# Column sums over half the rows: h's two row blocks added up ahead of TensorE, and the search's steps placed anew

## Time and profile before

| | |
|---|---|
| median of 3 runs | 497.21 us |
| the profiled execution | 497.13 us |
| its span, first to last instruction | 495.3 us |
| TensorE matmul busy | 476.9 us, 96% |
| VectorE busy | 371.3 us, 75% |
| GpSimd busy | 364.2 us, 74% |
| ScalarE busy | 354.4 us, 72% |
| DMA queue of SyncE, share of the 16 engines | 54.1% |
| granted TensorE clock | 1.00 |

### The profile page before, as it was taken

How to read it: one execution, slowest core, us unless ns; L and a number is a source line. 1 busy time by engine, 2 the same in 40 slices (tenths; PEclk the granted TensorE clock), 3 DMA queues, 4 the chain that set the end, 5 groups by cost and what they waited for, 6 DMA issues and landing times.

```text
span 495.3 us, 7476 instructions
## 1 busy us (share of the span) xinstructions
PE 476.9 (96%) x2442; PEld 327.1 (66%) x2442; DVE 371.3 (75%) x948; ACT 354.4 (72%) x727; POOL 364.2 (74%) x343
## 2 busy tenths in 40 slices
PE   1999999999999999999999999999999999999996
PEld 0256577667776777767776777757776677777774
DVE  5997898989887887789887897779876675533334
ACT  4767999877778777777788687768877665555652
POOL 0266569958789688868878687877879687797873
PEclk9999999999999999999999999999999999999999
DMA  8992556456566465646666266646444143444424
GB/s 320 339 411 90 225 199 238 148 217 245 214 236 255 171 243 214 238 164 267 255 254 253 94 263 253 245 180 243 185 179 168 76 163 128 158 171 169 171 85 169
DMA packets 27718, 102.75 MB, mean 207 GB/s; under 512 B 2080, under 2 KB 2592, under 8 KB 27680
## 3 DMA queue, kind: packets, MB, share of 16 engines
q1 hardware_dynamic: 27296, 101.23, 54.1%
q0 software_dynamic: 384, 1.05, 0.5%
HBM read 68.72 MB, written 33.55 MB: 206 GB/s over the span
## 4 chain that ended last, share of the span: by engine, by line
PE 82%; DVE 7%; ACT 4%; DMA 3%; issue 2%; POOL 1%; SPq 0%; DVEq 0%; ACTq 0%; POOLq 0%
PE ps L671 46%; PE ps L677 21%; PE aux L633 4%; PE ps L699 4%; PE aux L730 3%; DVE stats L804 2%; DMA xin<-x 2%; DVE res L986 1%; ACT hb L336 1%; PE aux L620 1%; PE aux L657 1%; DMA xg<-x_t,rows 1%; POOL h_lo L526 1%; PE aux L644 1%; ACT h_hi L372 1%
## 5 line engine op out<-in xcount | busy, mean ns | idle before, releaser
L537 POOL TENSOR_TENSOR r_lo<-r,r_hi 128x512 fp32r<-128x512 f32 x128 | 163.8, 1302 | 50.2 <-ACT r_hi L409 48.7
L526 POOL TENSOR_TENSOR h_lo<-hb,h_hi 128x512 fp32r<-128x512 f32 x128 | 164.3, 1297 | 7.3 <-ACT h_hi L372 7.3
L986 DVE SCALAR_TENSOR_TENSOR res<-ps,bias,res 128x512 f32<-128x512 f32 x128 | 90.0, 745 | 68.4 <-PE ps L706 68.4
L671 PE MATMUL ps<-r_hi,w_hi 128*128 128x512 f32 x256 | 108.0, 422 | 0.1
L671 PE MATMUL ps<-h_hi,w_hi 128*128 128x512 f32 x256 | 105.2, 411 | 0.5 <-DVE res L986 0.5
L671 PE MATMUL ps<-r_hi,w_lo 128*128 128x512 f32 x256 | 101.1, 395 | 0.0
L671 PE MATMUL ps<-h_hi,w_lo 128*128 128x512 f32 x256 | 101.1, 395 | 0.0
L336 ACT ACTIVATE hb<-xin,nmean,rstd 128x1024 f32<-128x1024 f32 x64 | 78.6, 1229 | 7.5 <-DVE nmean L825 7.3
L804 DVE BATCH_NORM_STATS2 stats<-xin 128x6 f32<-128x512 f32 x128 | 79.3, 677 | 4.1 <-DMA xin<-x 4.1
L392 ACT ACTIVATE r<-ps,beta 128x512 f32<-128x512 f32 x64 | 43.4, 684 | 53.2 <-PE ps L699 52.8
L386 ACT ACTIVATE r<-ps,beta 128x504 f32<-128x504 f32 x64 | 43.5, 679 | 51.6 <-PE ps L699 51.1
(11 more groups left out here) (101 smaller groups left out, 550.4 us busy)
## 6 DMA issues: line engine op xcount, KB each, us to landing
res<-x SPq DMA_DIRECT2D x32, 1024.0 KB, 4.9
out<-res SPq DMA_DIRECT2D x31, 1024.0 KB, 4.0
xin<-x SPq DMA_DIRECT2D x30, 1024.0 KB, 7.2
xin<-x SPq DMA_DIRECT2D x4, 512.0 KB, 5.4
out<-res SPq DMA_DIRECT2D x4, 256.0 KB, 2.1
w<-w_t SPq DMA_DIRECT2D x1, 256.0 KB, 9.5
cst<-small SPq DMA_DIRECT2D x1, 229.5 KB, 7.2
xg<-x_t,rows POOLq DMA_INDIRECT x8, 5.2
```

The source lines that it names most:

```text
L526: last = nc.gpsimd.tensor_tensor(h_lo[:, kf, n], hb[:, b % NH, kf, n], h_hi[:, kf, n].bitcast(F32), ALU.subtract)
L537: last = nc.gpsimd.tensor_tensor(r_lo[:, kf, n], r[:, kf, n], r_hi[:, kf, n].bitcast(F32), ALU.subtract)
L671: nc.tensor.matmul(bank[m][:], wt[:, kf, m * P:m * P + P], mov[:, kf, n], start=(kf == 0 and wt is w_hi), stop=False, skip_group_check=True)
L986: nc.vector.scalar_tensor_tensor(res[:, b % NR, m, n], bank[m][:], bias2[:, m:m + 1], res[:, b % NR, m, n], ALU.add, ALU.add).then_inc(out ...
```

## The change

- From group 3 on (`is_folded`), h's two row blocks are added up first, into a new tile `h_sum` [128, 4, 1024], and `column_sums` makes 16 matmuls on it where it made 32 on `hb`.
- For the first and the last batch of a group, VectorE adds the blocks (`add_blocks`, one 128x1024 fp32 instruction): the group's first batch in the third iteration, between `group_counts` and `moments`; its last batch in the first iteration of the next four, between `table` and `finish(t, 0)`.
- For the two in the middle, ScalarE writes h's first block a second time into `h_sum` (`write_twice`, ahead of `normalise` in the second and third iteration), and GpSimd issues a DMA that adds the second block to it in SBUF (`fold`, first thing in the third and fourth iteration).
- `column_sums` moves behind `layer2(t, 1)`, for all groups; `take_sums` moves behind `split_h(t+2, 0)`.
- `top_rows` moves from the end of the first iteration to the second, ahead of `finish(t, 0)`; `top_mark` behind that `finish`; `codes` moves from the second iteration to the third, ahead of `finish(t, 0)`, `group_onehot` to behind it.
- VectorE's `group_twin` goes; ScalarE's `twin` does both halves, in the third and the fourth iteration.
- `gather` moves from GpSimd's first iteration (last place) to the second, ahead of `split_h(t+2, 1)`. `transposes` and `spread_counts` move from the third to the fourth, and so does `group_gathered`.

```diff
--- before.py
+++ after.py
@@ -114,6 +114,7 @@
         r = sb("r", [P, KF, N])
         r_hi = sb("r_hi", [P, KF, N], F32R)
         r_lo = sb("r_lo", [P, KF, N], F32R)
+        h_sum = sb("h_sum", [P, G, N])
         fv = sb("fv", [P, N + 8])
         code = sb("code", [P, N], BF16)
         code_r = sb("code_r", [P, N], BF16)
@@ -208,6 +209,8 @@
         norm_ready = sem("norm_ready")
         h_part = sem("h_part")
         h_ready = sem("h_ready")
+        folded = sem("folded")
+        added = sem("added")
         fv_done = sem("fv_done")
         fv_copied = sem("fv_copied")
         static_ready = sem("static_ready")
@@ -260,6 +263,11 @@
             return k if (t + 1) % G == step and 1 < k < GROUPS else None
 
 
+
+        def is_folded(b):
+            return 3 * G <= b < NB
+
+
         def nth(b, h):
             return 2 * b + h + 1
 
@@ -393,6 +401,13 @@
                                                 accum_out=src2[:, m, e, NCLS:NSRC], **com)
                 last.then_inc(r_ready, 1)
 
+            def write_twice(b):
+                e = b % RB
+                act.wait_ge(norm_ready, b + 1)
+                act.wait_ge(fv_done, 2 * (b // G))
+                nc.scalar.activation(h_sum[:, b % G], xin[:, b % NX, 0], ACT.Relu, bias=nmean[:, 0, e:e + 1],
+                                     scale=rstd[:, 0, e:e + 1])
+
 
             def first_unit():
                 for m in range(KF):
@@ -487,11 +502,10 @@
                 relu(t + 1, 0, 0)
                 relu(t + 1, 0, 1)
                 split_r(t + 1, 0)
-                if group_at(t, 0) is not None:
-                    take_sums(group_at(t, 0))
                 if t + 2 < NB:
                     split_h(t + 2, 0)
                 if group_at(t, 0) is not None:
+                    take_sums(group_at(t, 0))
                     zeros(group_at(t, 0))
                 if t < NB - LEAD - 1:
                     root(t + LEAD + 1)
@@ -500,9 +514,15 @@
                 split_r(t + 1, 1)
                 if t + 2 < NB:
                     split_h(t + 2, 1)
+                if group_at(t, 2) is not None:
+                    twin(group_at(t, 2), 0)
                 if t + LEAD + 1 < NB:
+                    if t % G in (0, 1) and is_folded(t + LEAD + 1):
+                        write_twice(t + LEAD + 1)
                     normalise(t + LEAD + 1, 0)
                     normalise(t + LEAD + 1, 1)
+                if group_at(t, 3) is not None:
+                    twin(group_at(t, 3), 1)
 
         @block.gpsimd
         def _(pool):
@@ -537,6 +557,10 @@
                     last = nc.gpsimd.tensor_tensor(r_lo[:, kf, n], r[:, kf, n], r_hi[:, kf, n].bitcast(F32),
                                                    ALU.subtract)
                 last.then_inc(rlo_ready, 1)
+
+            def fold(b):
+                pool.wait_ge(h_ready, b + 1)
+                nc.gpsimd.dma_start(h_sum[:, b % G], hb[:, b % NH, 1], accum_op=ALU.add).then_inc(folded, 16)
 
             def gather(k):
                 pool.wait_ge(rows_ready, k + 1)
@@ -594,6 +618,8 @@
             for t in range(1, LAST):
                 if (t + 1) % G == 0:
                     tables((t + 1) // G)
+                if t % G in (1, 2) and is_folded(t + LEAD):
+                    fold(t + LEAD)
                 split_r(t + 1, 0)
                 if t < LAST - 1:
                     split_h(t + 2, 0, t + 1)
@@ -602,10 +628,10 @@
                 split_r(t + 1, 1)
                 if t == 1:
                     gather(1)
+                if group_at(t, 1) is not None:
+                    gather(group_at(t, 1))
                 if t + 2 < NB:
                     split_h(t + 2, 1)
-                if group_at(t, 0) is not None:
-                    gather(group_at(t, 0))
 
         @block.tensor
         def _(pe):
@@ -624,15 +650,22 @@
                                 last.then_inc(fv_done, 1)
 
             def column_sums(k):
-                pe.wait_ge(h_ready, G * k + G)
+                if is_folded(G * k):
+                    pe.wait_ge(folded, 32 * (k - 2))
+                    pe.wait_ge(added, 2 * (k - 2))
+                    blocks = 1
+                else:
+                    pe.wait_ge(h_ready, G * k + G)
+                    blocks = KF
                 pe.wait_ge(beta_ready, k)
                 for h in range(2):
                     n = half_of(h)
-                    for kf in range(KF):
+                    for kf in range(blocks):
                         for q in range(G):
+                            h_all = h_sum[:, q, n] if is_folded(G * k) else hb[:, (G * k + q) % NH, kf, n]
                             last = nc.tensor.matmul(
-                                aux[32 * q:32 * q + 32, n], c_("ones")[:, 0:32], hb[:, (G * k + q) % NH, kf, n],
-                                start=(kf == 0), stop=(kf == KF - 1), tile_position=(0, 32 * q))
+                                aux[32 * q:32 * q + 32, n], c_("ones")[:, 0:32], h_all,
+                                start=(kf == 0), stop=(kf == blocks - 1), tile_position=(0, 32 * q))
                     last.then_inc(fv_done, 1)
 
             def transposes(k):
@@ -773,15 +806,15 @@
                         class_values(1)
                     masks(t + 1, 0)
                     add_terms(t, 0)
-                    if group_at(t, 0) is not None:
-                        column_sums(group_at(t, 0))
                     layer2(t, 1)
                 else:
                     terms()
                     layer2(0, 1, lambda: add_terms(0, 0))
-                if group_at(t, 2) is not None:
-                    transposes(group_at(t, 2))
-                    spread_counts(group_at(t, 2))
+                if group_at(t, 0) is not None:
+                    column_sums(group_at(t, 0))
+                if group_at(t, 3) is not None:
+                    transposes(group_at(t, 3))
+                    spread_counts(group_at(t, 3))
                 layer1(t + 1, 1)
                 masks(t + 1, 1)
                 add_terms(t, 1)
@@ -884,11 +917,10 @@
                 nc.vector.tensor_scalar(cnt_d[:], c_("pick_n"), cnt[:], None, ALU.mult, ALU.add,
                                         accum_out=beside[:, 0:1]).then_inc(cntd_ready, 1)
 
-            def group_twin(k, i):
-                q = slice(64 * i, 64 * i + 64)
-                o = slice(64 - 64 * i, 128 - 64 * i)
-                nc.vector.tensor_scalar(onehot[o, k % 2, 1], code_r[q], c_("cls")[q], None, ALU.is_equal, ALU.add,
-                                        accum_out=beside[o, 1:2]).then_inc(onehot_ready, 1)
+            def add_blocks(b):
+                dve.wait_ge(h_ready, b + 1)
+                dve.wait_ge(fv_done, 2 * (b // G))
+                nc.vector.tensor_tensor(h_sum[:, b % G], hb[:, b % NH, 0], hb[:, b % NH, 1], ALU.add).then_inc(added, 1)
 
             def group_degrees(k):
                 gp = k % 2
@@ -1074,40 +1106,37 @@
                 table(t)
                 if t == 3:
                     group_biases(1)
-                if group_at(t - 1, 0) is not None:
-                    top_mark(group_at(t - 1, 0))
+                if t % G == G - 1 and is_folded(t + LEAD):
+                    add_blocks(t + LEAD)
+                if group_at(t, 1) is not None:
+                    top_rows(group_at(t, 1))
+                if group_at(t, 2) is not None:
+                    codes(group_at(t, 2))
                 finish(t, 0)
                 if group_at(t, 1) is not None:
-                    codes(group_at(t, 1))
+                    top_mark(group_at(t, 1))
                 if group_at(t, 2) is not None:
+                    group_onehot(group_at(t, 2))
                     group_counts(group_at(t, 2))
+                if t % G == 1 and is_folded(t + LEAD - 1):
+                    add_blocks(t + LEAD - 1)
                 if ahead < NB:
                     moments(ahead)
                 if group_at(t, 0) is not None:
                     top_first(group_at(t, 0))
                     top_next(group_at(t, 0))
                     top_best(group_at(t, 0))
-                if group_at(t, 2) is not None:
-                    group_twin(group_at(t, 2), 1)
                 if group_at(t, 3) is not None:
                     group_degrees(group_at(t, 3))
                     group_factors(group_at(t, 3))
+                    group_gathered(group_at(t, 3))
                 finish(t, 1)
                 if ahead < NB:
                     scales(ahead)
-                if group_at(t, 0) is not None:
-                    class_terms(t + 1)
-                    top_rows(group_at(t, 0))
-                if group_at(t, 1) is not None:
-                    group_onehot(group_at(t, 1))
                 if group_at(t, 3) is not None:
                     group_sources(group_at(t, 3))
-                if t + 1 < NB and group_at(t, 0) is None:
+                if t + 1 < NB:
                     class_terms(t + 1)
```

(4 more changed lines are left out.)

## The result

The changed kernel takes 520.76 us (519.25 to 521.15, 4 runs) against 497.26 us before; the ratio is 1.047, interval 1.0446 to 1.0494. I had put 494.2 us, with a range up to 499.0, and 0.18 on slower. The profiled execution took 519.25 us, its span 517.4 us, 22.1 us over the span before.

What follows compares the result with a forecast made beforehand. TensorE, busy 96% of the span, was taken as the bound. A saving of 9.0 us less stalls of 3.0, 2.5 and 0.6 gave -2.9 us, so 497.1 became 494.2 us, range 489.5 to 499.0.

Steps and rivals of the forecast that it cites:

- stall 2: Third iteration: VectorE work put ahead of `moments` delays root, relu and TensorE's class terms; 0.5 us, five times, 2.5 us.
- the rival's sum: Additions and GpSimd subtractions exclude each other on SBUF ports: 17 us stalls against 9 saved, 505 at worst; chance 0.11.
- Stall 1: First iteration: later column sums delay the search, `finish(t, 1)` and so the next layer 1; 0.5 us, six groups, 3.0 us.
- Stall 3: Second iteration: `top_rows` ahead of `finish(t, 0)` delays `layer1(t+1, 1)`; 0.1 us in each of 6 groups, 0.6 us.
- The saving: Half of the 32 column-sum matmuls leave TensorE: 1.8 us a group, 9.0 us for groups 3 to 7.
- What was covered: Second writes, twins, transfer issues, moved gather and transfer landings (5 to 10 us) were to fit in slack without stalls.

Runs made afterwards that it cites:

- one_input: Changed kernel with the third iteration's VectorE addition replaced by a same-size pass over the first block alone; 492.35 us, ratio 0.9909.
- pool_waits: Changed kernel with GpSimd waiting, in the third iteration, for the addition's semaphore before r's low part; 495.06 us, ratio 0.9967.
- best_late: three_transfers with `top_best`, the search's fourth pass, moved behind VectorE's `class_terms` in the first iteration; 489.44 us, ratio 0.9852.
- moves_only: Changed kernel with no group folded: 32 matmuls everywhere, no addition, second write or accumulating transfer, only the moved steps; 499.29 us, ratio 1.005.
- three_transfers: Changed kernel with the group's first batch also written twice and added by a transfer, so no third-iteration addition; 491.07 us, ratio 0.9882.
- wait_after_one: Changed kernel with GpSimd waiting for the addition between the two subtractions of r's low part in the third iteration; 506.62 us, one run.
- fold_behind: Changed kernel with the third iteration's accumulating transfer issued behind r's pair of subtractions instead of ahead of it; 510.25 us, ratio 1.028.

## Why the prediction was wrong

**The step that failed** is the price of `add_blocks` in stall 2, "I take 1.2", with an upper bound of 1.4 and "a stay of half a GpSimd instruction". It measured 6.44 us in four groups and 1.69 in one (t = 5). The mechanism was on the list of rivals, but mis-sized there too: "waits up to one GpSimd subtraction, 1.3 us". It waited for all that stood lined up, the rest of one piece and three more, 5.4 us. With third iterations 5.9 us longer in four groups and 0.7 in one, the rival's sum, with 3.6 for stalls 1 and 3, would be 488.1 + 3.6 + 23.6 + 0.7 = 516.0; the 4.4 us of the clock, which no rival had, make it 520.4. What I missed is that the pause in front of r's pair is not there any more: the gather moved ahead of h's pair fills it, so that five subtractions and two DMA issues follow one another. The pause before, and the gather after:

```profile
243.82 2.54 POOL L537 TENSOR_TENSOR r_lo<-r,r_hi 128x512 fp32r<-128x512 f32 x2 [1.83 <-ACT r_hi L409]
```

```profile
182.27 1.88 POOL L569 DMA_INDIRECT xg<-x_t,rows  x1
```

This part is read off the traces; no run puts the pause back with the addition at its place.

**A reading that was wrong**, and hid the size. I wrote that no VectorE instruction before reads two large tiles in SBUF, so that the rows can't show whether the two engines get in each other's way. `codes` does (L870, `fv` and `code`), and the trace before shows it, in its longest case and not in its median:

```profile
L870 DVE SCALAR_TENSOR_TENSOR code_r<-fv,code x8: 1205/1210/3018, 33.6 to 400.2; 128x1015 bf16<-128x1015 f32 x8
```

```profile
81.32 1.01 POOL L545 DMA_INDIRECT xg<-x_t,rows  x1
82.35 2.56 POOL L526 TENSOR_TENSOR h_lo<-hb,h_hi 128x512 fp32r<-128x512 f32 x2
82.97 3.02 DVE L870 SCALAR_TENSOR_TENSOR code_r<-fv,code 128x1015 bf16<-128x1015 f32 x1
...
84.86 3.53 POOL L537 TENSOR_TENSOR r_lo<-r,r_hi 128x512 fp32r<-128x512 f32 x2
```

Of eight instances seven meet no subtraction behind them and take 1.2 us. The one that starts inside h's pair, with a gather ahead of the pair, waits past a boundary and takes 3.02 us, and r's pair behind it is 1.0 us longer (3.53 for 2.54). In the changed kernel the same instruction takes 1.54 us in the third iterations, for the 1.21 that I put there.

**The Trainium skill's rule.** The Trainium skill, "SBUF — State Buffer", section "SBUF: two separate sides", has the exclusion of a two-input VectorE instruction and a GpSimd instruction that reads SBUF; one_input and pool_waits agree with that. It says that whoever starts first holds the ports for its instruction, which I took for a wait of one instruction at most. The runs differ: 3.96, 5.20, 6.44 and 7.93 us for one to four instructions let past, in the third iterations from t = 9 on, all with a DMA issue ahead. Here the measurement decides. The estimate of 1.22 us for the addition itself, by the formula of the Trainium skill's "VectorE: DVE Perf Modes" (section "The TRN2 errata — SBUF-src ops pay a fixed extra latency per instruction"), can't be told from the 1.08 to 1.3 us seen where the addition was let in.

**Stall 1** was right in its total and half right in its cause: 0.55 us an iteration measured, 0.5 predicted. In the changed kernel `finish(t, 1)` ends at 228.31 and the next layer's first weights load right behind it, after a pause:

```profile
228.42 0.19 PEld L704 LDWEIGHTS ps<-h_hi,w_hi 128*128 128x128 f32 x1 [0.45 <-issue]
```

best_late takes away 0.28 of the loss, which was the search's chain ahead of `finish`; the pause is not there. The other 0.28 stays when nothing waits; it comes with the sums at their new place, between two layers (moves_only has it too, 0.47 with the chain). What exactly it is was not tried.

**Stall 2 without the port** is the third iteration of one_input: 0.28 us, predicted 0.5; in pool_waits 0.8 with the wait for the subtraction. **Stall 3**: 0.00 to 0.02, predicted 0.1. **The saving** of 1.8 us a group is 1.70 by the first iterations of moves_only and three_transfers (17.03 and 15.33): 16 matmuls take 1.92 us, more than half of 3.64. The two kernels are 8.2 us apart, 9.0 put.

**What was covered** held: the second writes, twins and transfers cost nothing (three_transfers has no late third or fourth iteration with half as many again). An issue took 0.93 us, 1.03 put; a transfer landed in 5.7 us, 5 to 10 put. The gather, moved between subtractions, takes 1.88 us from t = 8 on for 1.03: it starts while `codes` is at work and ends 0.95 us after it. By itself that costs nothing (three_transfers has it too); what it does to the addition is told above.

**The clock** I had left out. Its 4.4 us come only with the long gaps: one_input and three_transfers have 14.47 in every fourth iteration. That it is the clock, wait_after_one shows: its third iterations are all 16.0 us, and the fourth ones behind them 15.92, 14.47, 15.99 and 14.48. Windows of 5 us in the first and the second of these (the granted clock is the third number from the end):

```profile
197.00:202.00 5.00, 5.00 (x20) 3.58 (x21) 2.76 (x7) 4.97 (x9) 4.68 (x5) 0.80 0.68 222
```

```profile
259.00:264.00 5.00, 5.00 (x29) 4.19 (x26) 4.73 (x11) 4.97 (x14) 3.45 (x4) 1.00 0.92 333
```

## What to carry to other kernels

Before a VectorE instruction with two SBUF inputs is placed beside a busy GpSimd, count how many SBUF-reading instructions stand ready on GpSimd's queue from there on, above all behind a DMA issue: that run, not one instruction, is the wait to price. Look in the trace at hand for such an instruction, small or large, and read its longest case beside its median. The wait can be ended on purpose, by a semaphore wait of GpSimd on the addition, which here bought 25 us for one line; cheaper still is to hand the second input to an accumulating DMA with enough iterations to land. Where a hand-over has little slack, the stall is priced twice, since TensorE comes back at the lower clock.

## What the runs showed of the hardware that was not expected

- GpSimd's subtractions shut VectorE's two-input addition out of one boundary or of several when a DMA issue of GpSimd (gather or accumulating transfer) stood ahead of them, up to 7.93 us, and let it in at the next boundary in 55 of 56 cases when none did: 1.6 us, against 3.7 us with a transfer ahead. best_late at t = 19 is the exception, 3.20 us.
- Left open: at t = 5 the addition was let in during the transfer's issue (1.69 us), at t = 9, 13, 17 and 21 it was not, though the pieces stand alike to 0.1 us. In fold_behind it was let in at t = 5 at the same boundary with no issue there (1.70 us). At t = 5 of these kernels h's pair started 0.01 to 0.02 us after the gather had ended, from t = 9 on at its end or before it; whether that decides was not tried. And in fold_behind it got in at such an issue after waiting past r's pair. What decides there was not found.
- After a stretch in which TensorE was idle most of the time (190 to 195 us) it was granted half its clock from 195 to 200 us, and the iteration behind such a stretch was 0.5 to 1.7 us longer. After the shorter gaps of wait_after_one the clock fell two times of four.
